# Attention inside a cross-attention and recurrent block: two steps as one TensorE unit, side work in a new order, one exp over both score tiles

## The reference, cut to what matters

```python
q, k, v = x @ Wq + bq, ctx @ Wk + bk, ctx @ Wv + bv    # 32 query heads, 8 key/value heads of 8 channels
attn = softmax(q k^T / sqrt(8) + mask)                 # 32 heads x 256 queries x 1601 keys
x0   = layer_norm((attn v) @ Wo + bo + x)
# RWKV-like block on x0: layer norm, token shift, five mixes through tanh(. @ w1) @ w2,
# decay w = exp(-exp(.)), r, k, v, g; a state of 8 x 8 per head is scanned over the 256 tokens;
# group norm, gate, @ Wo, residual x1; then a second layer norm and a feed-forward part
```

## Time and profile before

| | us |
|---|---|
| median of 3 runs (lowest, highest) | 1290.37 (1289.04, 1290.88) |
| the profiled execution | 1290.32 |
| its span, first to last instruction | 1288.5 |

### The profile page before, as it was taken

The page is one execution under the profiler, slowest core; times in us unless marked ns, Lnnn a source line. Parts: engine busy times, 40 slices in busy tenths (PEclk is TensorE's granted clock), DMA queues, the critical chain, the costliest instruction groups (busy, mean ns, idle before and its releaser), DMA issues.

```text
span 1288.5 us, 18192 instructions
## 1 busy us (share of the span) xinstructions
PE 1080.8 (84%) x7100; PEld 372.0 (29%) x7100; DVE 661.7 (51%) x1113; ACT 875.5 (68%) x953; POOL 366.3 (28%) x381
## 2 busy tenths in 40 slices
PE   3065999899899989999899989998999989997554
PEld 1011122232233323332233223331433223323312
DVE  5322141647463755556464746476465445454473
ACT  1045989777877777777877787777778877794001
POOL 6103023135111532144203522153213200340270
PEclk9567999999999999999999999999999989998666
DMA  5533405170514323261406141342306020500130
GB/s 186 136 92 114 94 1 141 45 128 2 131 34 101 58 91 66 70 97 46 94 26 131 28 125 40 83 76 92 65 11 97 3 40 11 75 1 1 19 55 10
DMA packets 65565, 87.47 MB, mean 68 GB/s; under 512 B 8208, under 2 KB 48192, under 8 KB 65472
## 3 DMA queue, kind: packets, MB, share of 16 engines
q1 hardware_dynamic: 63536, 82.91, 29.5%
q0 software_dynamic: 1936, 3.32, 0.9%
HBM read 50.74 MB, written 18.62 MB: 54 GB/s over the span
## 4 chain that ended last, share of the span: by engine, by line
PE 58%; ACT 14%; DVE 13%; issue 8%; POOL 3%; DMA 2%; SPq 2%; DVEq 0%; ACTq 0%; POOLq 0%
PE psum L702 56%; ACT probs L640 10%; DVE row_max L1124 3%; PE psum L800 1%; DVE o_raw L1171 1%; PE psum L794 1%; DVE k_c L1220 1%; POOL vs L532 1%; SPq L317 1%; DVE k_stack L1435 1%; DMA ctx_t<-in_mask 1%; ACT L640 1%; POOL vs L544 1%; DMA vs<-v_c 1%; DVE xa L1211 1%
## 5 line engine op out<-in xcount | busy, mean ns | idle before, releaser
L640 ACT ACTIVATE probs<-psum 128x1024 f32<-128x1024 f32 (+1 forms) x832 | 807.1, 1023 | 282.6 <-PE psum L702 279.0
L702 PE MATMUL psum<-probs,v_aug 128*9 128x512 f32 (+1 forms) x3328 | 446.8, 609 | 20.8 <-DVE o_raw L1171 20.6
L702 PE MATMUL psum<-q_stack,k_stack 64*128 64x512 bf16 (+1 forms) x1664 | 323.3, 396 | 49.3 <-ACT probs L640 39.9
L702 PEld LDWEIGHTS psum<-q_stack,k_stack 64*128 64x128 bf16 (+1 forms) x1664 | 83.2, 95 | 520.5 <-ACT probs L640 342.2
L527 POOL TENSOR_TENSOR xm<-tmp,xa 128x512 f32<-128x512 f32 x40 | 42.9, 1091 | 235.8 <-DVE tmp L1231 235.8
L1124 DVE TENSOR_REDUCE row_max<-psum 128x8 f32<-128x1024 f32 x64 | 78.0, 1218 | 53.9 <-PE psum L702 53.6
L544 POOL TENSOR_TENSOR vs<-r_c,vs 128x512 f32<-128x512 f32 x64 | 77.7, 1215 | 91.4 <-DVE vs L1242 91.4
L514 POOL TENSOR_TENSOR rstd<-moments,eps 128x2 f32<-128x2 f32 x24 | 4.9, 206 | 311.5 <-DVE moments L1197 311.5
L1242 DVE TENSOR_TENSOR_SCAN vs<-w_c,vs 128x514 f32<-128x514 f32 x64 | 88.9, 1389 | 3.5 <-POOL vs L532 1.1
L532 POOL TENSOR_TENSOR vs<-k_c,vs 128x512 f32<-128x512 f32 x64 | 83.4, 1308 | 23.6 <-DVE r_c L1373 15.0
L702 PEld LDWEIGHTS psum<-probs,v_aug 128*9 128x9 f32 (+1 forms) x3328 | 50.2, 88 | 126.5 <-issue 106.8
(11 more groups left out here) (175 smaller groups left out, 1134.6 us busy)
## 6 DMA issues: line engine op xcount, KB each, us to landing
vs<-v_c SPq DMA_DIRECT2D x64, 257.0 KB, 7.7
ctx_t<-in_mask SPq DMA_DIRECT2D x8, 1601.0 KB, 7.1
k_stacked<-k_parts SPq DMA_DIRECT2D x48, 200.1 KB
k_stack<-k_stacked SPq DMA_DIRECT2D x32, 300.2 KB, 6.5
ctx_t<-in_ctx_t SPq DMA_DIRECT2D x24, 400.0 KB, 5.0
q_stacked<-q_parts SPq DMA_DIRECT2D x96, 64.0 KB, 2.0
q_stack<-q_stacked SPq DMA_DIRECT2D x32, 192.0 KB, 6.7
ctx_t<-in_ctx_t SPq DMA_DIRECT2D x8, 401.0 KB, 3.3
```

What stands on the lines that cost most here:

```text
L640: nc.scalar.activation(probs[turn_step % NP][t][0:w, :, :], ps[t][0:w, :, :], ACT.Exp).then_inc(exped.sem, 1)
L702: return nc.tensor.matmul(dst, lhsT, rhs, start=start, stop=stop)
```

## The change

TensorE now takes two steps per pass of its loop. It writes both score tiles of an even step, does the small items due after the odd step before it (`score_rows`), weighs two steps, writes both score tiles of the odd step, and does `score_rows` and `side` of the even step. The second weighing of the units of steps 14 and 40 (`DIVIDED`) comes last in the unit. One exp reads all four score banks; so a score tile waits for the exp of the whole step before.

```diff
-        probs = [[sb(f"probs{n}{t}", [P, 2, 512]) for t in range(2)] for n in range(NP)]
+        probs = [sb(f"probs{n}", [P, 4, 512]) for n in range(NP)]
...
-            def exp_tile(b, step, t):
+            def exp_step(b, step):
                 turn_step = b * STEPS + step
-                if t == 0 and turn_step >= NP:
+                if turn_step >= NP:
                     act.wait_ge(weighed.sem, turn_step - NP + 1)
-                act.wait_ge(scored.sem, scored.at(b, 2 * step + t + 1))
+                act.wait_ge(scored.sem, scored.at(b, 2 * step + 2))
                 w = WIDTH[step % NC]
-                nc.scalar.activation(probs[turn_step % NP][t][0:w, :, :], ps[t][0:w, :, :], ACT.Exp).then_inc(exped.sem, 1)
+                nc.scalar.activation(probs[turn_step % NP][0:w, :, :], psum[0:w, 0:4, :], ACT.Exp).then_inc(exped.sem, 1)
...
                     for step in range(STEPS):
                         if b is not None:
-                            exp_tile(b, step, 0)
+                            exp_step(b, step)
                         side(step, c, d)
-                        if b is not None:
-                            exp_tile(b, step, 1)
...
             def score_tile(b, step, t, general):
-                pe.wait_ge(exped.sem, max(tile - 1, 0))
+                pe.wait_ge(exped.sem, b * STEPS + step)
...
-                    for step in range(STEPS):
+                    for step in range(0, STEPS, 2):
                         if b is not None:
                             score_tile(b, step, 0, general)
-                        if step >= 2 and b is not None:
+                            score_tile(b, step, 1, general)
+                        score_rows(step - 1, it, lo, general)
+                        if step == 0:
+                            if c is not None:
+                                weigh(c, STEPS - 2)
+                                weigh(c, STEPS - 1)
+                        elif b is not None:
                             weigh(b, step - 2)
-                        elif step < 2 and c is not None:
-                            weigh(c, STEPS - 2 + step)
+                            if step not in DIVIDED:
+                                weigh(b, step - 1)
                         if b is not None:
-                            score_tile(b, step, 1, general)
+                            score_tile(b, step + 1, 0, general)
+                            score_tile(b, step + 1, 1, general)
+                        score_rows(step, it, lo, general)
                         side(step, it, lo, general)
+                        if b is not None and step in DIVIDED:
+                            weigh(b, step - 1)
```

`score_rows` holds the rounds (steps 12 to 15 and 31 to 34), the two transposes of v (steps 3 and 7; 9 and 11 in turn 1), and the second decay product (step 21). `side` has all else, at even steps only, mostly two steps earlier than before and up to six in the recurrent part:

```diff
+DIVIDED = (NC + 1, 3 * NC + 1)
-KV_BANK = 5
-KV_STEP = [34, 36, 38, 40]
-A_ROUNDS = [35, 36, 37, 39]
+KV_BANK = (5, 5, 6, 7)
+KV_STEP = [32, 34, 42, 42]
+A_ROUNDS = [31, 32, 33, 34]
+B_ROUNDS = [12, 13, 14, 15]
```

The initial state moves from VectorE to GpSimd:

```diff
+            def first_state(c, j0):
+                for j in range(j0, j0 + HD // 2):
+                    pool.wait_ge(spread_in[j].sem, spread_in[j].at(c))
+                nc.gpsimd.tensor_copy(vs[:, j0:j0 + HD // 2, :, 0],
+                                      s_init[:, :, c % B, j0:j0 + HD // 2].rearrange("p e j -> p j e"))
...
             def state_pass(c, j):
-                dve.wait_ge(spread_in[j].sem, spread_in[j].at(c))
-                link(nc.vector.tensor_copy(vs[:, j, :, 0], s_init[:, :, c % B, j]))
                 dve.wait_ge(a_ready.sem, a_ready.at(c, j + 1))
```

More of the change, by code:

```diff
@@ L414, in all_turns @@
                                 load_x_rows(c)
-                        if step == 6 and a is not None:
+                        if step == 8 and a is not None:
                             if it == lo:
@@ L422, in all_turns @@
                             store_out(d)
-                        if general and step == 15 and b is not None:
+                        if general and step == 16 and b is not None:
                             full_masks(b, 1)
-                        if step == 16 and b is not None:
+                        if step == 18 and b is not None:
                             pass_shift(b, 1)
@@ L761, in score_tile @@
                 g, pair, w = group // 2, group % 2, WIDTH[c]
-                tile = b * TILES + 2 * step + t
                 if c == 0 and t == 0 and pair == 0:
@@ new lines, in score_rows @@
+                if a is not None:
+                    if step == (9 if it == lo else 3):
+                        if it == lo:
+                            pe.wait_ge(kv_biased.sem, kv_biased.at(a, 3))
+                        elif d is not None:
+                            pe.wait_ge(xa2_ready.sem, xa2_ready.at(d))
+                        else:
+                            pe.wait_ge(q_scaled.sem, q_scaled.at(a))
+                        turn_v(a, 0, 5 if it == lo else 7)
+                    elif step == (11 if it == lo else 7):
@@ L1019, in side @@
                             full_rounds(a, 0)
-                    elif step == 40:
-                        turn_shift(a, 0)
-                if f is not None and step in KV_STEP:
-                    n = KV_STEP.index(step)
-                    if n == 0:
-                        pe.wait_ge(o_normed.sem, o_normed.at(b, 2))
-                    else:
-                        pe.wait_ge(kv_biased.sem, kv_biased.at(f, n))
-                    project_kv(f, n, KV_BANK)
+                if b is not None and step in B_ROUNDS:
+                    r = B_ROUNDS.index(step)
+                    if r == 0:
+                        if d is not None:
+                            pe.wait_ge(ff_used.sem, ff_used.at(d))
+                            pe.wait_ge(rr_ready.sem, rr_ready.at(d))
+                        if a is not None:
+                            pe.wait_ge(v_kept.sem, v_kept.at(a))
+                            pe.wait_ge(q_scaled.sem, q_scaled.at(a))
+                    if not general:
+                        sub_round(b, 1, r)
+                    elif r == 3:
+                        full_rounds(b, 1)
@@ L1295, in all_turns @@
                     f, a, b, c, d = elements(it, lo)
-                    if a is not None:
-                        if it == lo:
-                            for n in range(NK):
-                                bias_kv(a, n, KV_SECOND[n])
-                        scale_q(a, 7 if it == lo else 6)
                     if d is not None:
                         scaled_rows(xn, x1, d, 2).then_inc(xn2_ready.sem, 1)
+                    if it == lo and a is not None:
+                        for n in range(NK):
+                            bias_kv(a, n, KV_SECOND[n])
+                        scale_q(a, 7)
+                        keep_v(a, 0, 5)
+                        keep_v(a, 1, 6)
+                        if not general:
+                            see_mask(a, 0)
+                            see_mask(a, 1)
                     if c is not None:
@@ L1321, in all_turns @@
                         row_moments(x0, c, 0)
-                    if a is not None:
-                        keep_v(a, 1, 7)
-                        if not general:
-                            see_mask(a, 0)
+                    if it > lo and a is not None:
+                        keep_v(a, 1, 6)
                     if c is not None:
@@ L1330, in all_turns @@
                         row_moments(x0, c, 1)
+                    if it > lo and a is not None and not general:
+                        see_mask(a, 0)
                     if it == B and not general:
@@ L1333, in all_turns @@
                         raise_flag()
+                    if c is not None:
+                        scaled_rows(xn, x0, c, 1).then_inc(xn_ready.sem, 1)
                     if d is not None:
                         write_out(d)
-                    if c is not None:
-                        scaled_rows(xn, x0, c, 1).then_inc(xn_ready.sem, 1)
                     if b is not None:
-                        for r in range(3):
-                            reduce_step(b, 1, r, general)
-                        keep_output(b, 0)
+                        reduce_step(b, 1, 0, general)
                     if c is not None:
```

466 lines of the change are left out of this document (246 added, 220 removed).

## The result

The changed kernel takes **1455.9 us** (1447.5 to 1460.3, 4 runs) against 1290.6 beside it: 1.1276 times as long, 95% interval 1.1223 to 1.1328. I had forecast 1341, in 1300 to 1385. It is slower, as forecast, but by 165 us and not by 51. The profiled execution has a span of 1455.3.

The account below looks back on a forecast made before the run. TensorE was taken to set the pace, with ScalarE waiting for it. Added times of 9 (turns 3 to 6), 7, 7, 7 (turns 2, 7, 8) and 20.6 us (turn 1) on 1290.3 gave 1341 us, range 1300 to 1385.

Parts of the forecast that it names:

- the turns' sum: Added time of all eight turns: 9 + 7 + 7 + 7 + 20.6 = 50.6 us on 1290.3.
- new waits on VectorE: Step 26's weighing waits for keep_output behind a scan; 1 us of cover found, taken at nothing, turns possibly few us longer.
- The loop, 2.58: Scores, one merged exp, next scores on one buffer: 2.58 us a step, ends 2.50 and 2.80; 416 steps make 1075.
- minus 0.055: Loop term: later score tile to exp takes 0.43 us, not 0.49, since its weights are already loaded.
- What does not fit behind the loop: Side work per full turn exceeding the loop: first halves 2.5, second halves 2.6, ScalarE 3.9, together 9.0 us.
- Rival 2: Loop is 2.58, but extras hide or are half, 4.5 us a turn: 1305 us, chance 0.11.
- TensorE waits more for VectorE than for ScalarE: Sign the forecast is wrong: the order of the side work decides, and not the loop.
- Rival 3: TensorE's clock falls in stretches with little side work: 80 us more, 1421, or half, 1381; chance 0.18.
- first_state: 64 small copies leave VectorE, two go to GpSimd; taken at nothing, after attention it might give or cost 2 us.
- Turn 1: Almost no side work, so pays the loop in full, plus a mask stall of 8.4: 150.7 us for 130.1.
- The two rules: Fewer tiling-mode changes save joins, alone 1249 us; against it, break up instructions of unsaturated engines that cause bubbles, which the forecast followed.
- Rivals 1, 2 and 4: First: TensorE stays last, grouping wins, 1266 us, chance 0.09. Second: see Rival 2. Last: exp costs 2.05, 1408 us, 0.04.

Follow-up runs that it names:

- e5: e2 with VectorE's state passes 4 to 7 each placed behind one of the four rounds' maxima: 1398.3 us, 1.0854 times the kernel before.
- e3: e2 plus zero-weight filler matmuls on TensorE in units with little side work: 1421.1 us, 1.1002 times the kernel before.
- e11: e5 plus zero-weight filler matmuls in second halves with little side work: 1377.7 us, 1.0664 times the kernel before.
- e2: The changed kernel with VectorE's gate and bonus moved to follow state pass 3, ahead of output normalisation and passes 4 to 6: 1455.6 us.
- e7: e6 with both mask reductions of turn 1 moved behind the rounds' maxima: 1297.4 us, 1.0059 times the kernel before.
- e10: e7 with the initial state copied on VectorE row by row again, instead of on GpSimd: 1293.6 us, 1.0021 times the kernel before.
- e9: The kernel before with only turn 1's first mask reduction moved behind the rounds' maxima: 1276.6 us, 0.9896 times the kernel before.
- e6: e5 with two exps a step and each score tile waiting for its own exp: 1308.7 us, 1.0151 times the kernel before.

## Why the prediction was wrong

**The step that failed is the turns' sum: it put new waits on VectorE at nothing ("I find 1 us of cover") and TensorE's clock at full speed past turn 1.** The first measured 8.4 us in each of six turns, the second 5.3 in turn 4. By turns, measured less forecast: turn 1 157.6 - 150.7 = 6.9; turn 2 14.5; turns 3 to 6 631.6 - 573.2 = 58.4; turn 7 15.4; turn 8 11.3; together 106.5. Behind the last exp 7.6 more (120.0 for 112.4), ahead of the first 0.8. That is the 115 us. Points 1 and 2 below are two errors that cancel, 3.1 us a turn too little and 3.6 too much; that they do is luck.

1. *The loop, 2.58.* It is 2.64. The exp was right, 1.88 for 1.89, and so was 0.215 for the second tile. Wrong was the "minus 0.055": from the later tile's start to the exp I took 0.43 since its weights were loaded. From the first tile's start (638.25) to the start of its exp (638.96) it is 0.71, which is 0.215 and the old 0.49; nothing is shortened. 0.055 x 416 = 23 us. The end of the range, 2.80, held it.
2. *"What does not fit behind the loop", 9.0 a turn.* In turn 4 those same extras come to 5.4 over 2.64 a step: the square root 2.55 (2.6 forecast), the mix 1.48 (2.0), the decay 0.6 (0.8), the rest 0.8 (3.6). I overcounted the first halves: a weighing pair takes 1.84 and not 1.96, from its start to the next scores, so each of 26 leaves 0.12 more. Rival 2 had the size of this term (4.5), though not the time. TensorE of the changed kernel:

```profile
612.56 1.90 PE L713 MATMUL psum<-probs,v_aug 128*9 128x512 f32 x16
614.40 0.61 PE L713 MATMUL psum<-q_stack,k_stack 64*128 64x512 bf16 x4
```

3. *"New waits on VectorE ... I find 1 us of cover".* This is the large one. I looked at `keep_output(b, 1)` and step 26, and asked of each moved VectorE instruction who waits for it, but not of the bonus: its place behind state pass 5 frees the bank of the first round for the next element, and the passes behind it hold the maxima that the second waits for. The step takes 11.0 and not 2.64: 8.4 in each of six turns, 50 us, with the half clock in it. e5 takes the passes out of the way and gives back 58. The forecast's "TensorE waits more for VectorE than for ScalarE, then the order of the side work decides" holds in this stretch, though not over the span, where its waits for exps are the longest. How the passes came to be so late, by GpSimd's copies, its products or the order alone, no run here separates.
4. *Rival 3, the clock, chance 0.18.* It was no rival but a second cause. In turn 4 steps 41, 46, 51 and 0 to 2 lie 5.3 us over 2.64, with weighing pairs of up to 2.94 for 1.90. I had priced it at 40 to 80; the filler, itself 58.6 us of TensorE, gives back 34 (e3) and 21 (e11). It comes on top of the stalls and partly from them, and each rival was priced alone on the forecast. The Trainium skill, TensorE: Matmul & The Clock Gate, A second HAM failure mode, tells of short idles that make the clock go to and fro. The traces agree, with 0.77 over the turn's start in e2 and 1.00 with the filler in e3.
5. *`first_state`, "it might give or cost 2".* The part behind the last exp grew by 7.6. The one copy for four rows on GpSimd wants the spreads of all four, where VectorE had copied row by row. Behind the last exp the product of `same` waited 13.62 (13.63 in e7, 6.40 in e10, 2.39 before); after, before and e10:

```profile
1398.71 2.08 PE L713 MATMUL psum<-tmp,same 128*128 128x512 f32 x2 [13.62 <-DVE tmp L1425]
```

```profile
1228.61 1.13 PE L702 MATMUL psum<-tmp,same 128*128 128x512 f32 x2 [2.39 <-DVE tmp L1377]
```

```profile
1233.05 2.07 PE L713 MATMUL psum<-tmp,same 128*128 128x512 f32 x2 [6.40 <-DVE tmp L1426]
```

   So copying row by row takes 7.2 off that wait, and 3.3 off the 6.2 us that e7 is longer than before behind its last exp. The rest of it isn't explained.
6. *Turn 1.* The forecast was 6.9 short, with wrong parts. The long step at the mask took 8.14, 5.5 over a plain one, where 8.4 and 3 behind it were forecast; the loop is 3 longer; steps 0 to 12 came to 7 over, for the 4 forecast; and later thin steps such as 22, 28, 30 and 48 took 3.9 to 4.1 at a granted clock near 0.6, 7.5 over in all, which is rival 3. The stall's cure (e7, e9) was in the earlier trace rows all along: a reduction that waits 15.37 for a transfer stands ahead of what TensorE waits for.
7. *The two rules.* Against the change stood the rule that, where ScalarE or VectorE isn't saturated but causes bubbles on other engines, breaking up its instructions may let work end sooner (the Trainium skill, Perfetto Trace Analysis, Optimizing Scalar/DVE Operations). The runs agree three times: 105, 90 and 80 us. The saved joins of the tiling rule are seen, 0.12 a pair in the weighing, and lie under the exp. Rivals 1, 2 and 4 are out as forecasts: steps of 2.64, stalls beyond the extras, an exp of 1.88.

## What to carry to other kernels

When two engines pass one buffer back and forth, one large instruction over both halves of it turns two overlapping loops into one that adds up; keep one instruction for each buffer, however idle its engine looks. When a list of an off-path engine is written anew, follow for each bank the last reader ahead of its next writer: two kinds of instruction of 0.7 and 1.2 us cost 50 us by what stood ahead of them, and moving the first alone gained nothing. And price causes together: a stall, and the lower clock behind it, were each in the profile, and only their sum was the answer.

## What was not expected of the hardware

- The granted clock fell within turns, in stretches with little side work. Over 14 us with TensorE busy 10.85 the granted clock was 0.76 (window of after, above); from 586 to 612, with a wait for the exp in each step too but TensorE busy 22.40 of 26, it was 1.00. Zero matmuls of 58.6 us made the kernel 34 us faster. Removing waits gave more: e6 has 0.931 without filler.
- VectorE's scans and GpSimd's products hold each other up where they run together. The scan takes 1389 ns on average before and 2055 after; GpSimd's products with k (L532, now L542) 1308 and 1547. The averages mix two levels. Before, 51 of the 64 scans overlap with no instruction of GpSimd and take 1.23 us; after, only 8 don't, at 1.21, and the other 56 take 2.18 on average. Before, scans start 2.7 to 5.8 us apart in the first five turns that have them, and GpSimd's product with r idles 91.4 us until a scan; after, they start 2.2 to 4.5 apart, 3.3 in the long step, and the product idles 0.0. The groups by form, before and then after:

```profile
L1242 DVE TENSOR_TENSOR_SCAN vs<-w_c,vs 128x514 f32<-128x514 f32 x64 | 88.9, 1389 | 3.5 <-POOL vs L532 1.1
L532 POOL TENSOR_TENSOR vs<-k_c,vs 128x512 f32<-128x512 f32 x64 | 83.4, 1308 | 23.6 <-DVE r_c L1373 15.0 <-DVE k_c L1366 4.5 <-DMA vs<-v_c 4.1
L544 POOL TENSOR_TENSOR vs<-r_c,vs 128x512 f32<-128x512 f32 x64 | 77.7, 1215 | 91.4 <-DVE vs L1242 91.4
```

```profile
L542 POOL TENSOR_TENSOR vs<-k_c,vs 128x512 f32<-128x512 f32 x64 | 98.7, 1547 | 27.1 <-DVE r_c L1420 23.6 <-DMA vs<-v_c 3.5
L557 POOL TENSOR_TENSOR vs<-r_c,vs 128x512 f32<-128x512 f32 x64 | 91.0, 1431 | 0.0
```

  GpSimd around the scan of 637.91, shown above:

```profile
637.84 1.18 POOL L557 TENSOR_TENSOR vs<-r_c,vs 128x512 f32<-128x512 f32 x1
638.98 2.19 POOL L542 TENSOR_TENSOR vs<-k_c,vs 128x512 f32<-128x512 f32 x1
```

  The product ends at 639.02 and the scan that began just behind it at 640.10, 1.08 later; the product that began during the scan ends at 641.17, 1.07 after the scan. So each seems to do its work only once the other is done. The Trainium skill, SBUF — State Buffer, Who interferes with whom, says that a VectorE instruction with two inputs in SBUF and a GpSimd instruction that reads SBUF contend, and calls it an exclusive lock. The traces agree; no run here took the products away from the scans to measure what it costs the kernel. VectorE of e5, with both levels:

```profile
605.15 2.28 DVE L1282 TENSOR_TENSOR_SCAN vs<-w_c,vs 128x514 f32<-128x514 f32 x1 [2.36 <-POOL vs L542]
...
607.93 1.21 DVE L1282 TENSOR_TENSOR_SCAN vs<-w_c,vs 128x514 f32<-128x514 f32 x1
```
